# Two square-block transposes on VectorE in place of TensorE's, with a later place for the gate sums, in a pre-norm decoder block

## The reference, cut to what matters

```python
def reference(x, ctx, ...):                     # x, ctx: 128 sequences x 128 tokens x 256
    x = x + self_attention(layernorm(x))        # one head; scores put through step bands, softmax, W_proj
    x = x + cross(layernorm(x), ctx, ctx)       # 8 heads of 32; gates by cumulative log-sigmoids, exp decay, group norm
    x = x + ffn(layernorm(x))                   # 256 -> 1024 -> 256, exact gelu, plus a rank-4 term from tokens of x
    return x

# ffn's second low-rank term, per sequence b: h . m2 with
m2 = even[:, 4:, :, None] * odd[:, 4:, None, :]   # four products of two tokens each, reshaped to 256 x 1024
out = h @ W2.T + scale * einsum('bsh,boh->bso', h, m2) + b2
```

## Time and profile before

| | |
|---|---|
| median of 3 runs | 2023.12 us (2022.67 to 2023.55) |
| the profiled execution | 2027.77 us |
| its span, first to last instruction | 2026.0 us |
| TensorE (PE) busy | 1940.2 us, 96% |
| VectorE (DVE) busy | 1522.6 us, 75% |
| ScalarE (ACT) busy | 1125.0 us, 56% |
| GpSimd (POOL) busy | 314.9 us, 16% |
| mean granted TensorE clock | 0.986 of full speed |

### The profile page before, as it was taken

The page is one execution under the profiler, slowest core; times in us unless marked ns, Lnnn a source line. Parts: engine busy times, 40 slices in busy tenths (PEclk is TensorE's granted clock), DMA queues, the critical chain, the costliest instruction groups (busy, mean ns, idle before and its releaser), DMA issues.

```text
span 2026.0 us, 47964 instructions
## 1 busy us (share of the span) xinstructions
PE 1940.2 (96%) x16404; PEld 1464.9 (72%) x16404; DVE 1522.6 (75%) x4318; ACT 1125.0 (56%) x2504; POOL 314.9 (16%) x257
## 2 busy tenths in 40 slices
PE   5789999999999999999999999999999999999988
PEld 4467777777777777777777777777777777777766
DVE  6577787778787778777778778777878777877742
ACT  2455566655556655556655556665555665555551
POOL 1111011111011111111111101111101111111110
PEclk9699999999999999999999999999999999999999
DMA  3000001110001111010110000011000111100000
GB/s 103 22 23 14 30 22 32 32 32 31 12 22 32 32 32 32 11 32 22 32 32 32 17 27 22 32 32 32 32 12 22 32 32 32 32 11 33 13 13 22
DMA packets 65583, 56.43 MB, mean 28 GB/s; under 512 B 13185, under 2 KB 65026, under 8 KB 65554
## 3 DMA queue, kind: packets, MB, share of 16 engines
q1 hardware_dynamic: 65554, 56.05, 8.9%
HBM read 37.15 MB, written 16.78 MB: 27 GB/s over the span
## 4 chain that ended last, share of the span: by engine, by line
PE 93%; DVE 4%; ACT 2%; issue 0%; DMA 0%; SPq 0%; DVEq 0%; ACTq 0%
PE UA L1290 16%; PE UB L1290 5%; PE TB L1232 5%; PE UB L1232 5%; PE UA L1232 5%; PE PV L1232 4%; PE UA L1240 3%; PE TA L1257 3%; PE TB L1372 3%; PE GT L1302 3%; PE TA L1372 3%; PE TA L1197 3%; PE TA L1101 3%; PE TB L1101 3%; PE QQ L1086 2%; PE UA L1310 2%
## 5 line engine op out<-in xcount | busy, mean ns | idle before, releaser
L1290 PE MATMUL UA<-W2f,hs_all 128*128 128x256 f32 x1536 | 349.1, 380 | 2.9 <-DVE ot L943 2.2
L1290 PEld LDWEIGHTS UA<-W2f,hs_all 128*128 128x128 f32 x1536 | 286.5, 190 | 62.3 <-issue 13.9
L957 DVE TENSOR_TENSOR C<-qT,QKs 128x512 f32<-128x512 f32 x256 | 169.3, 690 | 172.3 <-ACT qT L668 153.4
L550 POOL TENSOR_TENSOR Ng<-HT,gnw_b 128x256 f32<-128x256 f32 x128 | 94.9, 741 | 820.4 <-ACT HT L681 820.4
L531 POOL TENSOR_TENSOR xg<-x,gnb_b 128x1024 f32<-128x1024 f32 x32 | 75.9, 2372 | 811.1 <-DVE csum L893 811.1
L1290 PE MATMUL UB<-W2f,hs_all 128*128 128x256 f32 x512 | 115.8, 379 | 0.0
L659 ACT ACTIVATE hs_all<-UA,b1c 128x512 f32<-128x512 f32 x64 | 44.0, 687 | 109.6 <-PE TB L1240 109.6
L1290 PEld LDWEIGHTS UB<-W2f,hs_all 128*128 128x128 f32 x512 | 94.9, 190 | 11.7
L649 ACT ACTIVATE QKs<-TA 128x512 f32<-128x512 f32 x64 | 38.4, 600 | 108.9 <-PE DD L1257 108.9
L1257 PEld LDWEIGHTS TA<-xn2T,ctxT 32*128 32x128 f32 x512 | 63.2, 190 | 30.1 <-issue 27.7
L898 DVE TENSOR_SCALAR band_a<-sc 128x512 f32<-128x512 f32 x32 | 76.7, 2397 | 10.0 <-ACT sc L633 10.0
(11 more groups left out here) (311 smaller groups left out, 5532.3 us busy)
## 6 DMA issues: line engine op xcount, KB each, us to landing
xin<-x SPq DMA_DIRECT2D x32, 512.0 KB, 3.5
ctxn<-ctx SPq DMA_DIRECT2D x32, 512.0 KB, 3.8
out<-ot SPq DMA_DIRECT2D x32, 512.0 KB, 3.0
Ev<-xn SPq DMA_DIRECT2D x512, 1.0 KB
hs_all<-L_ffn_W SPq DMA_DIRECT2D x4, 512.0 KB, 8.7
T<-tok SPq DMA_DIRECT2D x128, 2.0 KB
moving<-parts SPq DMA_DIRECT2D x96, 8.0 KB, 1.9
QKs<-L_attn_W_qkv SPq DMA_DIRECT2D x1, 768.0 KB
```

The source lines that it names most:

```text
L550: pool.tensor_tensor(Ng[:, b, :].rearrange("p (k n) -> p k n", k=2), HT[:, b % 2, :, 0:P], gnw_b[:, :].rearrange("p (k n) -> p k n", k=2), ...
L957: dve.tensor_tensor(C[:, b % 2, 4 * hf:4 * hf + 4, :].rearrange("p h i -> p (h i)"), dx[hf], QKs[:, b, 4 * hf:4 * hf + 4, :].rearrange("p ...
L1290: ins = pe.matmul(OB[b][:, 0:D], hs_all[:, k, b * S:(b + 1) * S], W2f[:, k, :], start=(i == 0), stop=(i == KH - 1))
```

## The change

The context is loaded a second time, straight into `ctx_blocks` by eight DMAs of 32 partitions x 16 x 32 elements each, so that one VectorE transpose in 32x32 squares of 128x1024 elements gives `ctxT`. `xn1` is turned by VectorE in squares too (`block_xn1`), and sixteen DMAs inside the on-chip memory put the squares into `xn1T`, with the tokens in another order (slice, sequence, token); the scores and the copy of `qT` read that order. TensorE's `turn_xn1`, `turn_ctx` and ScalarE's four copies go. `low_rank` is now 8 products of 512 columns with one weight tile for all four sequences, and VectorE's `gT_copy` keeps each sequence's own rows by a mask `own_g`. `sums` moves behind the first adapter round. GpSimd's `xg` waits for `xn3l` instead of `csum`.

```diff
+        own_g = sb("own_g", [P, G])
+        sel_g = sb("sel_g", [P, G, CB * R])
-        sc = sb("sc", [P, N])
-        band_a = sb("band_a", [P, N])
-        band_b = sb("band_b", [P, N])
-        y = sb("y", [P, N])
+        sy = sb("sy", [P, 2, N])
+        sc, y = (sy[:, i, :] for i in range(2))
+        xn1_blocks = sy[:, :, :].rearrange("p k n -> p (k n)").rearrange("p (j n) -> p j n", j=HEADS)
+        bands = sb("bands", [P, 2, N])
+        band_a, band_b = (bands[:, i, :] for i in range(2))
+        ctx_blocks = bands[:, :, :].rearrange("p k (n c) -> p k n c", c=32)
-        Zo = sb("Zo", [P, KD, 40 * G])
+        Zo = sb("Zo", [P, KD, 32])
+        c_blocks = ctx_in.rearrange("(g b) (i a) d -> g a (b i) d", b=G, a=32)
...
+            def turn_xn1(it):
+
+                sp.wait_ge(blocks_ok.h, blocks_ok.at(it, 1))
+                sp.wait_ge(score_mm.h, score_mm.at(it, 1))
+                for i in range(4):
+                    for q in range(4):
+                        sp.dma_start(xn1T[32 * q:32 * q + 32, :, i * S:(i + 1) * S],
+                                     xn1_blocks[32 * i:32 * i + 32, q::4, :]).then_inc(xn1T_loaded.h, 16)
+
+            turn_xn1(-1)
...
                 if FFN.on(it):
                     ev_rows(it)
+                if SELF.on(it):
+                    sp.wait_ge(y_ok.h, y_ok.at(it, 1))
+                    for h in range(HEADS):
+                        sp.dma_start(ctx_blocks[32 * (h % 4):32 * (h % 4) + 32, h // 4, :, :],
+                                     c_blocks[it][:, :, 32 * h:32 * h + 32]).then_inc(blocks_loaded.h, 16)
+                if COMING.on(it):
+                    turn_xn1(it)
                 if CROSS.on(it):
                     e_rows(it)
...
-                    pool.wait_ge(csum_ok.h, csum_ok.at(it, 1))
+                    pool.wait_ge(xn3l_ok.h, xn3l_ok.at(it, 2))
...
+            def block_xn1(it):
+
+                dve.wait_ge(xn_ok[0].h, xn_ok[0].at(it, 1))
+                dve.wait_ge(PT_mm.h, PT_mm.at(it, 1))
+                dve.transpose(xn1_blocks.rearrange("p j (b a) -> p b j a", b=G),
+                              xn1[:, :, :].rearrange("p b (j c) -> p b j c", j=HEADS)).then_inc(blocks_ok.h, 1)
...
-                    dve.tensor_scalar(gT[:, :], GT[:, :], sc_b[:, 0:1], bias_row[:, 0:1], ALU.mult, ALU.add)\
-                       .then_inc(gT_ok.h, 1)
+                    dve.scalar_tensor_tensor(gT[:, :].rearrange("p (b s) -> p b s", b=G),
+                                             GT[:, :].rearrange("p (b s) -> p b s", b=G), bias_row[:, 0:1],
+                                             own_g[:, :].unsqueeze(2).broadcast_to([P, G, S]),
+                                             ALU.add, ALU.mult).then_inc(gT_ok.h, 1)
...
                 if cross:
                     head_sums(1)
                 if own:
+                    dve.wait_ge(blocks_loaded.h, blocks_loaded.at(it, HEADS * 16))
+                    dve.wait_ge(qk_mm.h, qk_mm.at(it, 2))
+                    dve.transpose(ctxT[:, :, :].rearrange("p k n -> p (k n)"),
+                                  bands[:, :, :].rearrange("p k n -> p (k n)")).then_inc(ctxT_ok.h, 1)
                     dve.wait_ge(probs_ok.h, probs_ok.at(it, 1))
                     link(dve.reciprocal(rinv[:, :], psums[:, :]))
...
             def project_q(it, m, k):
-                pe.wait_ge(xn1T_ok.h, xn1T_ok.at(it, 2))
+                pe.wait_ge(xn1T_loaded.h, xn1T_loaded.at(it, 16 * 16))
+                pe.wait_ge(x2_ok.h, x2_ok.at(it, G))
...
-                    elif i == 2 and cross:
-                        sums()
                 if ffn:
                     up_adapter(0)
+                if cross:
+                    sums()
...
-                    for b in range(G):
-                        tok_b = slice(b * S, (b + 1) * S)
-                        for k in range(KD):
-                            for c in range(CB):
-                                ins = pe.matmul(GT[32 * c:32 * c + 32, tok_b], Zo[:, k, 32 * b:32 * b + 32],
-                                                hs_all[:, KD * c + k, tok_b], start=(k == 0), stop=(k == 1))
+                    for k in range(KD):
+                        for c in range(CB):
+                            ins = pe.matmul(GT[32 * c:32 * c + 32, :], Zo[:, k, :], hs_all[:, KD * c + k, :],
+                                            start=(k == 0), stop=(k == 1))
...
-                if coming:
-                    turn_xn1(it)
-                if own:
-                    turn_ctx(it)
```

More of the change, by code:

```diff
@@ L301, in build @@
         raw_lo = sem("ffn_weights_rest")
+        xn1T_loaded = per_step("xn1T_loaded", COMING, 16 * 16)
         x_loaded = per_step("x_loaded", COMING, 16)
         ctx_loaded = per_step("ctx_loaded", SELF, 16)
+        blocks_loaded = per_step("blocks_loaded", SELF, HEADS * 16)
         e_loaded = per_step("e_loaded", CROSS, 16)
@@ L332, in build @@
         adapt_mm = per_step("adapt_mm", FFN, G)
-        xn1T_ok = per_step("xn1T_ok", COMING, 2)
-        ctxT_ok = per_step("ctxT_ok", SELF, 2)
+        blocks_ok = per_step("blocks_ok", COMING, 1)
+        ctxT_ok = per_step("ctxT_ok", SELF, 1)
         xn2T_ok = per_step("xn2T_ok", CROSS, 2)
@@ L518, in _ @@
                                base=-BIAS_ROW, pattern=[[-1, 1]], channel_multiplier=1)
+            v = sel_g[:, :, :].rearrange("p b (c r) -> p b c r", c=CB)
+            pool.affine_select(out=v, in_=v, compare_op=ALU.not_equal, fill=1.0, base=0,
+                               pattern=[[-8, G], [-32, CB], [-1, R]], channel_multiplier=1)
             for t in (WgT, Z, Zo, E, T, Ev, em):
@@ L571, in _ @@
             act.activation(rs0[0][:, :], lv[0][:, :], ACT.Exp, scale=-0.5).then_inc(rs0_ok[0].h, 1)
[L573 to L582, removed]
-                evac(it, xn1T_mm, xn1T_ok, TAB, xn1T, [score_mm])
             def evac_xn2T(it):
@@ L838, in _ @@
             dve.wait_ge(s_zero, 1)
+            done(dve.tensor_reduce(own_g[:, :], sel_g[:, :, :], AX_X, ALU.add))
+            done(dve.tensor_scalar(own_g[:, :], own_g[:, :], sc_b[:, 0:1], bias_row[:, 0:1], ALU.mult, ALU.add))
             dve.wait_ge(s_gbias, 16 * (2 * G + 1))
@@ L985, in apply0 @@
                     ln_apply(0, xin, xn1)
+                    block_xn1(it)
                 if coming:
@@ L1197, in score @@
                         ins = pe.matmul(TAB[0][:, b * S:(b + 1) * S], qT[:, k, b * S:(b + 1) * S],
-                                        xn1T[:, k, b * S:(b + 1) * S], start=(k == 0), stop=(k == 1))
+                                        xn1T[:, k, :].rearrange("p (i b a) -> p b i a", i=4, b=G)[:, b, :, :],
+                                        start=(k == 0), stop=(k == 1))
                     return ins
                 if ffn:
-                    transposes(it, xn3, [QQ, DD], xn3T_mm, [(xn_ok[2], 0)])
+                    transposes(it, xn3, [QQ, DD], xn3T_mm, [(xn_ok[2], 0), (dexp_ok, 0)])
                 if own:
```

27 lines of the change are left out of this document (10 added, 17 removed).

## The result

The changed kernel runs in 2105.43 us (median of 4, 2105.28 to 2106.75), the kernel before beside it in 2022.89 (2022.1 to 2023.55). The ratio is 1.041, with a 95% interval of 1.0392 to 1.0428. Forecast were 1984 us, 1950 to 2075 as the range, and 0.60 for faster: the sign was wrong and the range did not hold the time. The profiled execution has a span of 2103.2 us, 77.2 longer than that of before.

What follows compares the result with a forecast made beforehand. TensorE's order was taken to bound the kernel. Per step -2.6 us of work and +1.3 of waiting at `project_q` gave -1.3, 31 times -40, setup costing 1: together -40, median 1984 us, whole range 1950 to 2075.

Steps and rivals of the forecast that it cites:

- What bounds the kernel: Whole loop: TensorE, busy 1940.2 of 2026.0 us; every microsecond off its order shortens the step until an awaited input is late.
- The work removed: TensorE's order, per step: 1.75 us of transposes, 0.76 for `sums`, 0.1 for `low_rank`, together 2.6 us gained.
- The transposes: TensorE ahead of `down(2)`: removing the 16 transposes gains 1.75 us per step; ScalarE's four copies behind them are worth nothing.
- The late sums: TensorE behind the adapter round: `sums` fills the wait for gelu, 0.76 us gained per step, its readers not held longer.
- The chain to `project_q`: `C` products, norm's apply, square transpose, sixteen SP transfers, landing: `project_q` on TensorE waits 1.3 us (0 to 3.3) per step.
- the issue of the sixteen transfers: SP's queue ahead of `project_q`: 0.48 us each, ends 0.39 and 0.61; the last begins 7.2 us after the first.
- Start: Setup: sixteen issues ahead of nine small loads, landing at 26.6, and two mask operations; costs 1 us.
- Context pieces late: Rival, chance 0.15: 128-byte context pieces cost as much as 1 KB packets, `pv(3)` waits 6.2; +5.2 us per step, 2185.
- Squares at half speed: Rival, chance 0.17: VectorE's square transpose takes 2.46 us, `project_q` waits 2.8; +1.2 us per step, 2060.
- Issue hidden: Rival, chance 0.15: SP issues at 0.39 us, `project_q` doesn't wait, 0.6 us wait for Z; -2.0 us per step, 1961.
- The range: Total time: 1950 to 2045 us by the ends of issue cost and `low_rank`; whole range 1950 to 2075, without late context pieces.

## Why the prediction was wrong, point by point

1. **What bounds the kernel.** Right. TensorE's order set the step, and nearly all the time taken from it came back where nothing else was late (0.8 us of a step for the context alone, 0.7 for the sums alone, 1.8 for both with the norm on TensorE).
2. **The work removed.** 2.6 us a step were forecast; the step without a fall of the clock shows 2.45. The transposes were right. The late sums were right only together with GpSimd's earlier start, which I had put at nothing: it is worth 10 us. The reader of the sums that I had not followed up is TensorE itself, in the products behind `up(4)`; with the sums moved alone it waits 0.24 us for them. `low_rank` was put at 0.1 us gained and is worth nothing.
3. **The chain to `project_q`.** The mechanism and all its terms but one were right: squares 1.23 us (measured 1.23 and 1.25), the last `C` products in time for `pv(3)`, landing 1.9 us, `project_q` due 1.75 us earlier. **The step that failed is the issue of the sixteen transfers**: 0.48 us each, between the large load's 0.39 and the Ev rows' 0.55, measured 0.646, above even my upper end of 0.61. Fifteen times the difference is 2.5 us, and so the wait was 3.55 us where I had 1.3. The nearest rows were those of copies within the chip's memory, `moving` at 0.61 above all, and I took a value below them because 32 partitions lie between the forms; no row showed that the issue goes by partitions. With 0.61 I would have forecast a wait of 3.3 us and a step longer than before, but still only 2045 us.
4. **The granted clock.** Missing altogether. The kernel before has only one wait of 0.76 us in a loop step and its clock never falls there; a wait of 3.5 us on the engine that bounds the kernel is a new thing, and I priced it at its own length. It cost 3.55 us and on average 1.4 more. The forecast step was 1.3 us shorter than before, the measured one is 2.5 longer; of these 3.8 us the longer wait makes 2.25, the clock 1.4, and the work removed the rest.
5. **Start.** I had 1 us for the setup and nothing for the first two steps. There TensorE has only a part of its work between the norm's apply and `project_q`, and the waits are 8.0 and 11.2 us.
6. **The rivals.** Context pieces late: refuted. The eight loads land 2.0 us after issue, some three microseconds before VectorE wants them. The low price of small packets was the right end: with the context part alone the queue's packets took 14.2% of 16 x 1999.2 us instead of 8.9% of 16 x 2026, for 135,168 packets more, which gives an estimate of 12 ns each, where I had 8 and the rival needed 33. The page "DMA: Bandwidth & Descriptors" of the Trainium skill says in "Specifications" that pieces below 512 bytes are read, modified and written; whatever that adds, it was hidden here. Squares at half speed: refuted, and with it the estimate by which eight of the 311 ns that the Trainium skill's page "VectorE: DVE Perf Modes" states in "The three transpose paths" are 2.5 us; 1.23 us were measured for 128x1024 in 32 bits. The section "Rules for kernel authors" of that page of the Trainium skill leaves full transposes to TensorE. The context went against that and gained 23 us, its squares having been put in place by the load; `xn1`, whose squares had to be put in order afterwards, takes the same time on TensorE (1966.68 us) and on VectorE with two queues (1967.0), and loses with one queue. The measured slope, +2.5 us a step, lies between those of the two slow rivals, +1.2 and +5.2, and has neither's cause. Issue hidden: one issue never was that short, but two queues made it true in effect, at a step of 58.0 us, and with no wait for `Z`.
7. **The range.** The ends of my own terms do not give the 1950 to 2045 that I wrote for the forecast: no wait and 0.2 for `low_rank` is -2.7 us a step and 1940 us, a wait of 3.3 and 0.3 lost is +1.1 and 2058. The measured time lies outside these too.

What stays open: why a transfer of 32 x 2 x 128 elements within the chip's memory costs 0.646 us to issue and a context load of 32 x 16 x 32 from HBM 0.51, though it moves eight times as many pieces; and why the clock falls in two of three steps after the same idle time. Neither was tried further.

## What to carry to other kernels

Where many small DMAs replace one engine's work, add up the issues on the queue first: their number times the dearest row of their kind (here 0.65 us) is a serial chain, and it belongs on two queues or under 10 us of other work. On the engine that sets the time, price a new wait of some microseconds at more than its length, and look in the windows behind it for the granted clock; filling it with idle work is the test. When two edits come together, one of them "for nothing", take it out alone before calling it nothing.

## What the runs showed of the hardware

- A square-block transpose of 128x1024 32-bit elements on VectorE takes 1.23 us, as long as an add of that size.
- Issuing costs 0.64 to 0.67 us for each of these transfers on SP and on ScalarE's queue alike, and the two go on side by side.
- With 3.5 us of idle time in each step TensorE's granted clock fell to 0.50 for 3.4 us in one step of three and for 6.8 us in another, and did not fall in the third. With transposes of the identity in that time, or with a wait of 0.25 us in its place, it stayed at 1.00.
- A scan on VectorE beside GpSimd's add took 2.63 us where it takes 0.42 without it, and an operation on 128x512 elements 2.46 where it takes 0.41.
- `low_rank` in 16 turns of four column groups with 128 columns and in 4 turns with 512 takes the same time, 1.89 and 1.86 us.
- Sixteen semaphore increments in a row held ScalarE's queue long enough to be seen: with one in their place TensorE's two waits for it were 1.6 us together instead of 4.0 (an estimate of 0.08 us for each increment left out), and the kernel was 7 us shorter.
